# Residual of all eight groups on DVE, with x loaded into SBUF a second time and no adding transfers

## The chip, the cores and the metric

The kernel runs on one core of a Trainium2 chip. Its time is the device time of one execution in microseconds (us); the median of several executions is compared. Profiles come from one execution each. The engines are TensorE (PE in the rows), VectorE (DVE), ScalarE (ACT), GpSimd (POOL) and SyncE (SP), which here only issues transfers.

## What is computed

The input x is 4 sequences of 512 tokens with 256 channels, f32. It is normalised, goes through a recurrent attention layer (RWKV: the WKV scan over time) and a mixture of 16 experts of which each token uses 4, and the product of both is added to x:

```python
x = L0_attn_hidden                    # (4, 512, 256)
xn = _layernorm(x, axis=-1)
s = _L0_attn_ref(xn, ...)             # k, v, r = projections of mixed xn; s = (r * wkv) @ Wo.T
g = _silu(_L0_ffn_ref(xn, ...))       # sum over the 4 chosen experts of coeff * (silu(x Wg) * (x Wu)) @ Wd
x = x + s * g
```

## The kernel before

**Stages.** x is loaded and normalised in SBUF (in the room of `rT`), stored as rows to DRAM (`xn_rows`), projected to k, v and r (`kT`, `vT`, `rT`), and routed: a table says which row of which token goes to which expert and in which order. Then the loop over units of 256 rows runs. `NEED` = 32 units always, up to 14 more by the counts; here 36 run. For one unit i:

- POOL gathers 2 x 128 rows from `xn_rows` (`gather`, line 388) and, `LAG` = 6 units behind, scatters 2 x 128 finished rows into `y_rows` (`scatter`, line 395). `y_rows` has one section for each of a token's four chosen experts, called slots.
- TensorE transposes the rows (`transpose_x`), makes gate and up products (`gate_up`) and the down products of an earlier unit (`down`). `product` is line 584, so all of these have that line in the profile.
- ScalarE copies out the transposed rows (`evac_x`), applies Silu (`silu`, line 534), loads the weights of the next unit's expert (`load_weights`, line 442) and copies y (`evac_y`, line 544). `evac_y(i)` waits until the scatter of unit i - 2 from the same buffer has landed (`y_out`). After eight units (`EXPS_AT`) it also does one Exp of 128x2048 for WKV, between `evac_x` and `silu` of its step.
- DVE multiplies gate and up (`hidden`, line 1022) and in between works off the WKV scan in pieces (`WKV_AT`); the last piece is done in step 29. `wkv_ready` counts the eight pieces (4 sequences x 2 halves of the channels).

k's room is free for other data once the WKV of its columns is done; `xre` are eight views of [128, 2, 256] into `kT`, one for each group of two token tiles.

**The end.** For each token the four slots are read back from `y_rows` into `y4` and summed with their weights into `acc`. The reads are issued by SP in order: slot 0 in one transfer (line 304), slot 1 in halves (308), slot 2 in quarters (313), slot 3 in eighths (321), each as soon as the counts say that its rows have been scattered. DVE sums: slot 0 at line 1087, the others at 1089, through `weighted` and `summed`; the `hidden` of the last two units stand between the sums of slots 0 and 1. After the last read, for each of the eight groups n: DVE adds slot 3 (`weighted(n, 3)`), ScalarE applies Silu (line 577), DVE multiplies by s, which TensorE left in PSUM (`gated`, line 1119).

x is added in two ways. Groups 0 to 5 (`ADDED`): early in the loop, after two WKV pieces, SP copies their x from the input to the output in DRAM (line 294), and at the end POOL stores `acc` with transfers that add to what is there (line 431). Groups 6 and 7 (`SUMMED`): SP loads their x into `xre` behind the reads of slot 2 (line 316), DVE adds it (`residual`, line 1126), and SP stores the result (line 324). The kernel ends when both kinds of stores have landed (lines 325 and 326).

## Time and profile before

| | |
|---|---|
| median of 3 executions | 328.44 us (327.49 to 329.75) |
| the profiled execution | 325.01 us |
| its span, first to last instruction | 323.3 us |
| busy: PE, PEld, DVE, ACT, POOL | 286.9, 210.9, 250.4, 146.1, 202.8 us |
| DMA | 63.27 MB, mean 196 GB/s |
| mean granted TensorE clock | 0.98 |

The span is the time between the first and the last instruction in the profile of one execution. An engine's busy share of it is an average over stages with different limits; which engine sets the end in a stage is read from its idle time and from who ends it. "Landing" is the time from the issue of a transfer to its completion.

### The profile page before, as it was taken

To read this page: it belongs to the slowest core of one execution; us is meant where nothing else is said; L and a number is where in the kernel's file an instruction comes from. 1 tells how busy PE (TensorE), PEld (TensorE's weight loads), DVE (VectorE), ACT (ScalarE), POOL (GpSimd) and SP (SyncE) were. 2 spreads that over 40 slices of the span, in tenths; PEclk is the share of its full clock that TensorE was granted. 3 is DMA by queue.
4 is the path that set the end of the run, shared out by engine and by line. 5 is a ranking of instruction groups with operands and counts; after the bars stand their busy time and mean duration, and the time that the engine had idled before them with its cause. 6 is when DMAs were issued, how large, how long until landed. Compare 5 with 4: busy or idle time off the path is not lost.

```text
span 323.3 us, 4531 instructions
## 1 busy us (share of the span) xinstructions
PE 286.9 (89%) x1298; PEld 210.9 (65%) x1299; DVE 250.4 (77%) x516; ACT 146.1 (45%) x219; POOL 202.8 (63%) x201
## 2 busy tenths in 40 slices
PE   0698969999899999999899999999999999998910
PEld 0433424444346657888788888888888888887800
DVE  2979799997886897697399886989869941196993
ACT  1792735423266934932836428273292323211040
POOL 3600079994872777587787777778777775425071
PEclk9999979999999999999999999999999999999995
DMA  7896000016298785677654646556465666996999
GB/s 234 278 396 266 0 1 1 0 57 230 86 262 269 277 290 152 215 222 255 194 188 148 209 138 207 182 170 205 149 214 158 167 223 183 388 300 216 307 213 180
DMA packets 30346, 63.27 MB, mean 196 GB/s; under 512 B 4300, under 2 KB 20173, under 8 KB 30160
## 3 DMA queue, kind: packets, MB, share of 16 engines
q10 hardware_dynamic: 7568, 23.88, 22.0%
q0 software_dynamic: 8544, 19.41, 21.4%
q1 hardware_dynamic: 14208, 19.66, 17.7%
q8 instruction: 13, 0.21, 0.3%
q14 instruction: 13, 0.11, 0.1%
HBM read 50.35 MB, written 15.20 MB: 203 GB/s over the span
## 4 chain that ended last, share of the span: by engine, by line
PE 62%; DVE 18%; DMA 10%; issue 4%; POOL 3%; ACT 1%; ACTq 0%; DVEq 0%; POOLq 0%; SPq 0%
PE ps L584 54%; PE ps L691 4%; DMA y_rows<-arena,late 4%; DVE arena L842 3%; DMA rows<-y_rows 3%; POOL arena L388 3%; DVE arena L1089 3%; DVE ohB L993 2%; PE ps L594 2%; DVE ohA L988 2%; DMA arena<-xn_rows,tok_idx 2%; DMA wrou<-wrouT_in 2%; DVE arena L1119 1%; PE ps L709 1%; DVE rows L817 1%
## 5 line engine op out<-in xcount | busy, mean ns | idle before, releaser
L584 PE MATMUL ps<-arena,rows 128*128 128x256 f32 x448 | 101.5, 380 | 0.7 <-issue 0.7
L388 POOL DMA_INDIRECT arena<-xn_rows,tok_idx x72 | 78.2, 1086 | 25.7 <-issue 21.7
L584 PEld LDWEIGHTS ps<-arena,rows 128*128 128x128 f32 x448 | 82.9, 190 | 11.4 <-issue 1.3
L395 POOL DMA_INDIRECT y_rows<-arena,dst_idx x60 | 66.6, 1110 | 25.7 <-issue 16.5
L584 PE MATMUL ps<-wdn,arena 128*128 x288 | 68.1, 380 | 2.4 <-DVE arena L1022 2.4
L584 PEld LDWEIGHTS ps<-wdn,arena 128*128 128x128 f32 x288 | 54.0, 190 | 10.2 <-issue 3.2
L584 PE MATMUL ps<-arena 128*128 128x512 f32 x96 | 47.2, 626 | 3.1 <-DVE arena L842 3.1
L544 ACT COPY arena<-ps 128x512 f32<-128x512 f32 x34 | 19.9, 587 | 64.1 <-PE ps L584 57.8
L370 POOL TENSOR_SCALAR ohB<-late 128x128 f16<-128x128 f32 x20 | 29.9, 1508 | 27.9 <-DVE late L918 27.3
L1022 DVE TENSOR_TENSOR arena<-arena,ps 128x512 f32<-128x512 f32 x28 | 19.1, 684 | 34.3 <-PE ps L584 15.0
L534 ACT ACTIVATE arena<-ps 128x512 f32<-128x512 f32 x36 | 21.5, 598 | 30.9 <-PE ps L584 30.8
L584 PEld LDWEIGHTS ps<-arena 128*128 128x128 f32 x96 | 17.4, 196 | 19.5 <-issue 15.2
L584 PE MATMUL ps<-rows,arena 128*128 128x512 f32 x64 | 29.0, 595 | 0.9 <-issue 0.7
L526 ACT COPY arena<-ps 128x512 f32<-128x512 f32 x36 | 21.5, 596 | 5.5 <-PE ps L691 5.0
L1089 DVE SCALAR_TENSOR_TENSOR arena<-rows,coef,arena 128x256 f32<-128x256 f32 x48 | 20.1, 480 | 3.7 <-DMA rows<-y_rows 3.6
L691 PE MATMUL ps<-ident,arena 128*128 128x128 f32 x144 | 21.6, 274 | 1.3 <-DMA arena<-xn_rows,tok_idx 1.3
L691 PEld LDWEIGHTS ps<-ident,arena 128*128 128x128 f32 x144 | 17.8, 141 | 6.2 <-issue 2.0
L584 PEld LDWEIGHTS ps<-rows,arena 128*128 128x128 f32 x64 | 11.5, 190 | 12.8 <-issue 12.1
L842 DVE SCALAR_TENSOR_TENSOR arena<-arena,vec 128x512 f32<-128x512 f32 x24 | 16.9, 742 | 0.0
L594 PE MATMUL ps<-ident,rT 128*128 128x128 f32 x32 | 6.8, 358 | 10.6 <-ACT rT L457 10.6
L474 ACT ACTIVATE arena<-arena,late 128x512 f32<-128x512 f32 x24 | 15.7, 718 | 0.0
L395 POOL DMA_INDIRECT y_rows<-arena,late x8 | 8.0, 1000 | 12.1 <-ACT arena L544 10.0
(179 smaller groups left out, 371.0 us busy)
## 6 DMA issues: line engine op xcount, KB each, us to landing
rows<-wgu_in ACTq DMA_DIRECT2D x44, 512.0 KB, 4.0
wdn<-wd_in SPq DMA_DIRECT2D x1, 4096.0 KB, 13.9
rT<-x_in SPq DMA_DIRECT2D x4, 512.0 KB, 6.0
xn_rows<-rT SPq DMA_DIRECT2D x4, 512.0 KB, 3.5
rows<-y_rows SPq DMA_DIRECT2D x1, 2048.0 KB, 10.6
rows<-y_rows SPq DMA_DIRECT2D x2, 1024.0 KB, 8.1
rows<-y_rows SPq DMA_DIRECT2D x4, 512.0 KB, 7.5
rows<-y_rows SPq DMA_DIRECT2D x8, 256.0 KB, 4.4
```

What stands on the lines that cost most here:

```text
L370: ins = pool.tensor_scalar(ohB[:, t % RING, s], iota_row, prow[:, t, s:s + 1], val[:, 1 - s % 2, t:t + 1], ALU.is_equal, ALU.mult)
L388: pool.indirect_dma_start(out=xg[i % XG][:, j, :], out_offset=None, in_=xn_rows, in_offset=bass.IndirectOffsetOnAxis(ap=tok_idx[:, 2 * i + ...
L395: pool.indirect_dma_start(out=y_rows, in_=ysb[:, par, j, :], in_offset=None, out_offset=bass.IndirectOffsetOnAxis(ap=idx[:, n + j:n + j + ...
L474: ins = nc.scalar.activation(mix[b % 2][w][:, c, :], xnT[:, c, b, 0:SEQ], ACT.Copy, scale=unmix[:, w * C + c:w * C + c + 1])
L526: nc.scalar.copy(xTg[:, i % 2].rearrange("p c t -> p (c t)"), ps[:, XT_BANK[i % 2], :]).then_inc(xt_ready, 1)
L534: nc.scalar.activation(dst, src, ACT.Silu).then_inc(sg_ready, 1)
L544: nc.scalar.copy(ysb[:, par].rearrange("p j n -> p (j n)"), ps[:, Y_BANK[par], :]).then_inc(y_ready, 1)
L584: ins = nc.tensor.matmul(dst, lhsT(c), rhs(c), start=(c == 0), stop=(c == C - 1))
L691: ins = nc.tensor.transpose(ps[:, XT_BANK[i % 2], (c * 2 + j) * P:(c * 2 + j + 1) * P], xg[i % XG][:, j, c * P:(c + 1) * P], ident[:, :])
L842: ins = V.scalar_tensor_tensor(out=mix[b % 2][w][:, c, :], in0=xnT[:, c, b, 1:SEQ + 1], scalar=vec[:, (2 + w) * C + c:(2 + w) * C + c + 1] ...
L1022: V.tensor_tensor(hT[:, par].rearrange("p h t -> p (h t)"), sg[:, par], ps[:, B_G + 2 * par + 1, :], ALU.mult).then_inc(h_ready, 1)
L1089: ins = V.scalar_tensor_tensor(out=acc[:, t, :], in0=y4[:, t, k, :], scalar=coef4[:, t, k:k + 1], in1=acc[:, t, :], op0=ALU.mult, op1=ALU.add)
```

## The change

- SP no longer copies x to the output. In the loop it now waits until all eight WKV pieces are done and then loads x of all eight groups into `xre` (eight transfers of 256 KB), ahead of the reads of slots 0 to 3. The loads of groups 6 and 7 behind slot 2 go.
- The counts are read into SP's registers ahead of this wait; the wait for WKV ahead of the reads of slot 2 goes, since the same wait now stands earlier.
- POOL does no adding transfers. DVE does `residual` for all groups, that of group n - 2 behind `gated(n - 1)`, and SP stores each of the eight groups when its residual is done.

```diff
--- before.py
+++ after.py
@@ -195,7 +195,7 @@
         LAST_Y_BANK = [(Y_BANK[FIRST % 2], B_XT), (Y_BANK[(FIRST - 1) % 2], B_HT)]
         XN_BANK = [(B_XT, B_Y), (B_HT, B_G + 3)]
         S_BANK = [B_G, B_G + 1, B_G + 2, B_G + 3, B_XT, B_HT, B_R, B_Y]
-        ADDED, SUMMED, QUARTERS = range(6), range(6, T // 2), 4
+        QUARTERS = 4
         logits = ps[:, B_R, 0:T * E].rearrange("p (t e) -> p t e", t=T)
         LG_BANK = [B_G, B_G + 1, B_G, B_G + 2]
         prefix = ps[:, B_Y, 0:(T + 1) * E].rearrange("p (t e) -> p t e", t=T + 1)
@@ -244,7 +244,7 @@
         xre_in = sem("xre_in")
         acc_ready, silu_ready, s_psum, ffn_times_s, res_ready = (
             sem("acc_ready"), sem("silu_ready"), sem("s_psum"), sem("ffn_times_s"), sem("res_ready"))
-        out_stored, out_added, x_in_out = sem("out_stored"), sem("out_added"), sem("x_in_out")
+        out_stored = sem("out_stored")
 
         def wait(eng, s, value):
 
@@ -289,14 +289,13 @@
             sp.dma_start(wdn[:, :, :, :].rearrange("p c e n -> p (c e n)"), wd_in).then_inc(wdn_in, 16)
             sp.wait_ge(slots_known, 3)
 
-            sp.wait_ge(wkv_ready, C)
-            halves = lambda a: a.rearrange("b s d -> (b s) d")[0:len(ADDED) * 2 * P]
-            sp.dma_start(halves(out), halves(x_in)).then_inc(x_in_out, 16)
-
             counts = [sp.value_load(slot_done[0:1, n:n + 1], min_val=1, max_val=32 * (NP // 2 + 1))
                       for n in range(2 * (TOPK - 1))]
             scattered = [sp.value_load(used[0:1, 3 + par:4 + par], min_val=32 * (NEED // 2), max_val=32 * (NP // 2 + 1))
                          for par in range(2)]
+            sp.wait_ge(wkv_ready, C * BATCH)
+            for n in range(T // 2):
+                sp.dma_start(xre[n], out_order(x_in)[:, 2 * n:2 * n + 2, :]).then_inc(xre_in, 16)
             for s in range(TOPK - 1):
                 for par in range(2):
                     sp.wait_ge(y_out[par], counts[2 * s + par])
@@ -307,23 +306,19 @@
                         tt = slice(q * T // 2, (q + 1) * T // 2)
                         sp.dma_start(y4[:, tt, s, :], y_v[:, tt, s, :]).then_inc(y_second_in[q], 16)
                 else:
-                    sp.wait_ge(wkv_ready, C * BATCH)
                     for q in range(QUARTERS):
                         tt = slice(q * TB, (q + 1) * TB)
                         sp.dma_start(y4[:, tt, s, :], y_v[:, tt, s, :]).then_inc(y_third_in[q], 16)
 
-            for n in SUMMED:
-                sp.dma_start(xre[n], out_order(x_in)[:, 2 * n:2 * n + 2, :]).then_inc(xre_in, 16)
             sp.wait_ge(last_y_psum, 2 * 2)
             for par in range(2):
                 sp.wait_ge(y_out[par], scattered[par])
             for n in range(T // 2):
                 sp.dma_start(y4[:, 2 * n:2 * n + 2, TOPK - 1, :], y_v[:, 2 * n:2 * n + 2, TOPK - 1, :]).then_inc(y_last_in[n], 16)
-            for n in SUMMED:
-                sp.wait_ge(res_ready, n - SUMMED[0] + 1)
+            for n in range(T // 2):
+                sp.wait_ge(res_ready, n + 1)
                 sp.dma_start(out_v[:, 2 * n:2 * n + 2, :], acc[:, 2 * n:2 * n + 2, :]).then_inc(out_stored, 16)
-            sp.wait_ge(out_stored, 16 * len(SUMMED))
-            sp.wait_ge(out_added, 16 * len(ADDED))
+            sp.wait_ge(out_stored, 16 * (T // 2))
 
         @block.gpsimd
         def _(pool):
@@ -424,11 +419,6 @@
                     pool.indirect_dma_start(out=y_rows, in_=ysb[:, (FIRST + n) % 2, j, :], in_offset=None,
                                             out_offset=bass.IndirectOffsetOnAxis(ap=e_idx[:, column:column + 1], axis=0),
                                             bounds_check=last_row, oob_is_err=False).then_inc(y_out[(FIRST + n) % 2], 16)
-
-            pool.wait_ge(x_in_out, 16)
-            for n in ADDED:
-                pool.wait_ge(ffn_times_s, n + 1)
-                pool.dma_start(out_v[:, 2 * n:2 * n + 2, :], acc[:, 2 * n:2 * n + 2, :], accum_op=ALU.add).then_inc(out_added, 16)
 
         @block.scalar
         def _(act):
@@ -1122,7 +1112,7 @@
             def residual(n):
                 tt = slice(2 * n, 2 * n + 2)
                 dve.wait_ge(ffn_times_s, n + 1)
-                dve.wait_ge(xre_in, 16 * len(SUMMED))
+                dve.wait_ge(xre_in, 16 * (T // 2))
                 V.tensor_tensor(acc[:, tt, :], acc[:, tt, :], xre[n], ALU.add).then_inc(res_ready, 1)
 
             for n in groups:
@@ -1130,7 +1120,7 @@
                 weighted(n, TOPK - 1).then_inc(acc_ready, 1)
                 if n > 0:
                     gated(n - 1)
-                if n - 2 in SUMMED:
+                if n > 1:
                     residual(n - 2)
             residual(T // 2 - 2)
             gated(T // 2 - 1)
```

## Rows read from the trace of the kernel before

**Rows 1.** The page, part 4: chain that ended last, by engine

```profile
PE 62%; DVE 18%; DMA 10%; issue 4%; POOL 3%; ACT 1%; ACTq 0%; DVEq 0%; POOLq 0%; SPq 0%
```

**Rows 2.** Timeline of TensorE: start us, us, operation, count [idle before <-releaser]

```profile
146.66 1.89 PE L584 MATMUL ps<-wdn,arena 128*128 x8
...
159.25 1.99 PE L584 MATMUL ps<-wdn,arena 128*128 x8 [1.18 <-DVE arena L1022]
...
273.89 3.62 PE L584 MATMUL ps<-arena,rows 128*128 128x256 f32 x16
...
280.19 3.69 PE L584 MATMUL ps<-arena,rows 128*128 128x256 f32 x16 [0.52 <-issue]
```

**Rows 3.** Timeline of ScalarE, its copy of y (line 544) near 152 us

```profile
152.12 0.58 ACT L544 COPY arena<-ps 128x512 f32<-128x512 f32 x1 [6.39 <-DMA y_rows<-arena,dst_idx]
```

**Rows 4.** Line 395 (scatters), issued 120 to 140, then 142 to 145 us: landing

```profile
DMA to landing us min/median/max: 2.4/2.7/3.2
...
DMA to landing us min/median/max: 7.7/7.9/8.0
```

**Rows 5.** Timeline of SP's queue, whole span: issues (issue time, not landing)

```profile
141.37 0.63 SPq L294 DMA_DIRECT2D out<-x_in  x1
...
271.58 0.37 SPq L304 DMA_DIRECT2D rows<-y_rows  x1
...
292.58 2.61 SPq L313 DMA_DIRECT2D rows<-y_rows  x4
295.23 2.71 SPq L316 DMA_DIRECT2D kT<-x_in  x2
```

**Rows 6.** Timeline of DVE: end of WKV, weighted sums, last groups

```profile
260.52 0.69 DVE L1072 TENSOR_TENSOR rT<-arena,rT 128x512 f32<-128x512 f32 x1
...
286.99 0.69 DVE L1022 TENSOR_TENSOR arena<-arena,ps 128x512 f32<-128x512 f32 x1 [0.30 <-DVE arena L1087]
...
288.15 3.26 DVE L1089 SCALAR_TENSOR_TENSOR arena<-rows,coef,arena 128x256 f32<-128x256 f32 x8 [0.47 <-DMA rows<-y_rows]
...
298.49 6.83 DVE L1089 SCALAR_TENSOR_TENSOR arena<-rows,coef,arena 128x256 f32<-128x256 f32 x16 [2.95 <-DMA rows<-y_rows]
...
305.51 1.67 DVE L1089 SCALAR_TENSOR_TENSOR arena<-rows,coef,arena 128x256 f32<-128x256 f32 x4 [0.18 <-DMA rows<-y_rows]
...
309.09 0.88 DVE L1089 SCALAR_TENSOR_TENSOR arena<-rows,coef,arena 128x256 f32<-128x256 f32 x2
...
310.48 0.87 DVE L1089 SCALAR_TENSOR_TENSOR arena<-rows,coef,arena 128x256 f32<-128x256 f32 x2
...
316.15 0.69 DVE L1126 TENSOR_TENSOR arena<-arena,kT 128x512 f32<-128x512 f32 x1
...
316.76 0.68 DVE L1119 TENSOR_TENSOR arena<-arena,ps 128x512 f32<-128x512 f32 x1
...
317.47 0.69 DVE L1126 TENSOR_TENSOR arena<-arena,kT 128x512 f32<-128x512 f32 x1
```

**Rows 7.** Waits of SP's queue: us in total, times, longest

```profile
SPq L56 <- DMA out<-arena: 1.2, 1, 1.2
```

**Rows 8.** Landings: line 304; 442 at 267 and 272.6 us; 324; 288

```profile
rows<-y_rows SPq DMA_DIRECT2D x1, 2048.0 KB, 10.6
...
DMA to landing us min/median/max: 4.0/4.0/4.0
...
DMA to landing us min/median/max: 7.5/7.5/7.5
...
DMA to landing us min/median/max: 4.0/4.3/4.6
...
DMA to landing us min/median/max: 2.9/3.5/4.1
```

**Rows 9.** Stretches by engine: busy (x instructions), PEclk, DMA share, GB/s

```profile
266.00:270.00 4.00, 4.00 (x22) 3.52 (x21) 0.69 (x1) 1.07 (x2) 2.77 (x4) 1.00 0.63 196
...
278.00:282.00 4.00, 3.48 (x19) 2.89 (x18) 0.29 (x1) 1.07 (x2) 1.04 (x2) 1.00 1.06 385
```

## The prediction

> **What bounds the kernel now.** I read the page first: its part 4 puts TensorE on the path for most of the span, 62% of the chain that ended last [rows 1]. So I split the time in two. Through the expert loop, up to about 280 us, what moves TensorE moves the end. After that the chain hands over to DVE, and there I read the timeline of DVE and of SP's queue.
>
> The reader is to see three things. First, TensorE has almost no idle time in the loop. One of its gaps is the 1.18 us before the down products at 159.25 us, released by DVE line 1022 [rows 2]. Following that wait backwards: `hidden` waited for ScalarE's Silu, and ScalarE had stood still for 6.39 us before its copy of y at 152.12 us, released by a scatter into `y_rows` [rows 3]. An Exp (`EXPS_AT`) then came between that copy and the Silu. The two scatters issued from 142.4 us landed after 7.7 and 8.0 us, where those of the 20 us before needed 2.4 to 3.2 [rows 4]. What was new is the copy of x to `out`, issued at 141.37 us [rows 5].
>
> Second, at the end DVE is full. The third term's sums start at 298.49 us, when their first quarter lands, and run 6.83 us to 305.3; after that one group follows the other every 1.39 us (309.09 to 310.48), which is its two weighted sums and its gating and nothing else. Only groups 6 and 7 have a residual there, and the last ends at 317.47 + 0.69 = 318.16 us [rows 6].
>
> Third, what follows is SP's: its last wait for a store takes 1.2 us [rows 7]. I take it for that of group 7, which lands 4.0 us after its issue [rows 8], at about 318.2 + 4.0 = 322.2 of the 323.3 us. Then the adding transfers are over before it and end nothing.
>
> **The change, part by part.** *Copy of x removed.* The 1.5 MB from x to `out` at 141.37 us goes. The wait of ScalarE behind the scatter was what held the loop up, and scatters of 2.4 to 3.2 us would have landed by 147.5 us, ahead of the y product that the copy of y needs, done at 146.66 + 1.89 = 148.55 us [rows 2]. So the 1.18 us of TensorE come back, and since it then runs without a gap until about 280 us, all later work comes earlier by it: **-1.2 us**. Bounds: 0, if something else on ScalarE's way held it as long; the whole gap, rounded up, -1.3. That POOL's scatters move with TensorE I assume.
>
> *Six more residuals on DVE.* POOL's six adding transfers go; DVE does six more `tensor_tensor` of 128x512 f32. The trace has the same operation twice, 0.69 us each [rows 6]. In a chain with no wait, though, the next instruction starts before the former has ended: the gating at 316.76 starts 0.61 us after the residual at 316.15, and 1.39 less two weighted sums of 3.26/8 = 0.41 us each leaves 0.57 us for a gating [rows 6]. I take 0.60 us: 6 x 0.60 = 3.6 us. Nothing hides it, DVE being full from 298.5 us on. From this goes 0.1 us, because residual(6) no longer stands right behind the gating that it needs: **+3.5 us**. Bounds 3.4 (six of 0.57) and 4.1 (six of 0.69). The Trainium skill (VectorE: DVE Perf Modes, The TRN2 errata) gives a fp32 `tensor_tensor` (N + 151)/0.96 ns, 691 ns for 512 elements, and says that SBUF latency is exposed between instructions; by that the term would be 4.1 us, the sum 0.6 us more. The 0.69 of single instructions here agrees, the spacing does not, and I go by the spacing.
>
> *x loaded earlier.* All eight groups (2 MB, eight issues) now go out once WKV is done, 260.52 + 0.69 = 261.2 us, ahead of the read of the first term, which was issued at 271.58 us [rows 5, 6]. Both move earlier with TensorE, so the room of 10.4 us stays. Eight issues take 8 x 1.36 = 10.8 us if each is as slow as the two of line 316, and 8 x 0.65 = 5.2 us by the four of line 313 [rows 5]. So SP is hardly late. What is queued behind on SP is the reads of the first, second and third term and then of the last. As to the engines: between 266 and 270 us the DMA moves 196 GB/s at a share of 0.63, and 385 at 1.06 when it is full [rows 9], so some 189 GB/s are free, and 2.1 MB need 11.1 us. About 1 us of backlog is left when the first term's read is issued. That read's landing after 10.6 us, at 282.2 [rows 8], lets DVE end `hidden` at 286.99 + 0.69 = 287.7, 0.47 us ahead of the second term's first half [rows 6], so half of it is slack. The rest is given back at the end, where 0.5 MB of x no longer lie between the third term and the last scatters (0.5 MB at 385 GB/s is 1.4 us).
>
> The weight loads feel it too. In the loop a load lands after 4.0 us, but the one issued at 272.6 us, beside the first term's read, took 7.5 [rows 8]: it landed at 280.1, and TensorE started its products at 280.19 us after 0.52 us idle [rows 2]. The one before, issued at 267.0 us for the products at 273.89, has 6.9 us; with x in the way as the first term was, it lands 0.6 us late: **+0.6 us**. Bounds: 0 (the x loads are over, or take only spare bandwidth) and 2.0 (0.6 for each of two loads and 0.8 on the first term's read).
>
> *x loads gone from 295.23 us.* They stood behind the third term on the same queue, so they delayed no sum of it. The last term's first read can come sooner, but DVE is busy until 305.3 us anyway; DVE's next sum started at 305.51, 0.2 us after it [rows 6]: **-0.1 us**, bounds -0.2 and 0.
>
> *Stores.* Each group goes out on SP when its residual is done, now one per 1.39 + 0.60 = 2.0 us. The last still follows the last residual. Before, it landed after 4.0 us beside adding transfers; the kernel's other stores, 512 KB to `xn_rows`, land after 2.9 to 4.1 us, median 3.5 [rows 8]. I take 3.3 us: **-0.7 us**; bounds -1.1 (2.9) and +0.6 (4.6, the other store of line 324). The Trainium skill (DMA: Bandwidth & Descriptors, Anatomy of one DMA) gives 2.0 us and bytes/436e3 for a DMA issued from GpSimd: 2.6 us for 256 KB, an estimate by which this term were -1.4 and the sum 0.7 us less. No store of this trace is that quick.
>
> Sum: -1.2 + 3.5 + 0.6 - 0.1 - 0.7 = +2.1 us. On the profiled execution's 325.01 us (a span of 323.3 and 1.7 around it) that is 327.1. The median shown, 328.44, is 3.4 us above the profiled one; the same +2.1 on it gives 330.5 us. Own range of this case, with the copy's term kept near -1.2: the low ends add up to +0.8; the high ones would make +5.5, but they hardly come together, and the largest of them (2.0 instead of 0.6) with half of the next (0.6) makes +4.1: 329.2 to 332.5.
>
> **The rivals.** *The stall stays (no gain from the copy's removal).* Against it speaks that the long landings begin with the copy; for it, that the wait was found in one execution only. Then +2.1 + 1.2 = +3.3, 331.7 us.
>
> *x ahead of the first term holds up the sums: slower.* Place: SP's queue at 272 us. If the eight issues take 10.8 us and the engines serve weights and scatters in turn with x, the first term's read begins 2 to 3 us late. Its sums, `hidden` of the last unit but one, the second term's first half, `hidden` of the last unit, its down products and its scatter follow each other on DVE and TensorE [rows 6]. Of a landing 2.9 us late 0.5 is slack and the last scatter's easier way gives back 0.6: 1.8 us more, +3.9, 332.3 us. It decides (over 1%, 3.3 us) from 1.2 us handed on, a landing 1.7 us late with nothing given back. For it: the full DMA from 274 us on, in which the first term's 2 MB take 10.6 us. Against it: 10.4 us of room.
>
> *The copy cost more than the profiled execution shows.* Once ScalarE's Silu is late, every further us of the scatters' landing is a us of TensorE, and the runs shown are 3.4 us slower than the profiled one. If 3 us come back: +0.3, 328.7 us; with a quicker last store it is faster than before.
>
> **How the numbers follow.** Forecast 0.60, the stall that stays 0.12, x ahead of the first term 0.18, the dearer copy 0.10. About 1% (3.3 us) is what a measurement of this kernel can tell from no change, its three runs being 2.3 us apart. Slower by over 1%: 0.05 of the forecast, half of the first rival, 0.15 of the second, together 0.26. Faster by over 1%: 0.04, all from the third. The rest, 0.70, is within 1%. The range runs from the third rival's lighter side, 328.0, to the second's heavier, 333.4, with a tenth or so left out in all.
>
> **What would show it.** In the profile after: no idle of ScalarE over 1 us for a scatter near 150 us, and no gap of TensorE at 158; scatters there land in about 3 us. DVE's groups at the end 2.0 us apart and eight residuals, with no wait for x between. The last residual ends at about 318.16 - 1.2 + 3.5 + 0.5 = 321.0 us. SP's x issues from about 260 us, the first term's read 10 us behind, one TensorE gap of about 0.5 us more near 273. A last store that lands in 3.3 us. The prediction is wrong if TensorE has new gaps of more than 1 us, if the first term lands over 1.7 us later relative to TensorE's steps, or if the residuals cost less than 0.5 us each because DVE waits for reads of the last term.

## The result, and the profile after

| | before | after |
|---|---|---|
| median of 18 executions each | 327.9 us (325.85 to 330.97) | 330.35 us (328.29 to 332.59) |
| ratio after / before | | 1.0097, 95% interval 1.0072 to 1.0122 |
| profiled execution's span | 323.3 us | 326.9 us |

The change makes the kernel slower by just under 1%. The ratios and their intervals, here and below, compare only executions of the faster of two groups that the executions of one kernel fall into, so they are not the quotients of the medians, which take in all; the profiles of early_copy and pe6_spread are of slower executions.

The forecast, 330.5 us, was met in the median. The rows below show that this is partly luck: the stores gained about 2 us more than forecast, the copy and the loads of x together did about 1 us worse, and about 0.9 us of the difference lies where the forecast has no term.

At the end, DVE's timeline of the kernel after (start us, us, operation, count, what ended the idle time before). Line 1079 is the weighted sum, 1109 the gating, 1116 the residual; they answer to lines 1089, 1119 and 1126 in [rows 6].

```profile
307.68 1.72 DVE L1079 SCALAR_TENSOR_TENSOR arena<-rows,coef,arena 128x256 f32<-128x256 f32 x4 [0.88 <-DMA rows<-y_rows]
...
310.35 0.88 DVE L1079 SCALAR_TENSOR_TENSOR arena<-rows,coef,arena 128x256 f32<-128x256 f32 x2 [0.35 <-DMA rows<-y_rows]
...
312.35 0.88 DVE L1079 SCALAR_TENSOR_TENSOR arena<-rows,coef,arena 128x256 f32<-128x256 f32 x2
313.14 0.68 DVE L1109 TENSOR_TENSOR arena<-arena,ps 128x512 f32<-128x512 f32 x1
313.74 0.68 DVE L1116 TENSOR_TENSOR arena<-arena,kT 128x512 f32<-128x512 f32 x1
314.34 0.87 DVE L1079 SCALAR_TENSOR_TENSOR arena<-rows,coef,arena 128x256 f32<-128x256 f32 x2
...
323.62 0.69 DVE L1116 TENSOR_TENSOR arena<-arena,kT 128x512 f32<-128x512 f32 x1
```

The groups now follow each other every 1.99 us (312.35 to 314.34), 0.60 us more than before, and the last residual ends at 324.31 us.

SP's last wait and the landing of its eight stores, after (the page's list of issues: count, KB each, median us to landing):

```profile
SPq L56 <- DMA out<-arena: 1.8, 1, 1.8
```
```profile
out<-arena SPq DMA_DIRECT2D x8, 256.0 KB, 2.1
```

The span ends 326.9 - 324.31 = 2.6 us after the last residual. In [rows 6, 7] it is 323.3 - 318.16 = 5.1 us.

TensorE's timeline after, near the place of the old gap, and at the last units:

```profile
159.93 1.89 PE L574 MATMUL ps<-wdn,arena 128*128 x8
...
274.50 3.69 PE L574 MATMUL ps<-arena,rows 128*128 128x256 f32 x16
...
287.57 3.71 PE L574 MATMUL ps<-arena,rows 128*128 128x256 f32 x16 [2.04 <-issue]
292.90 1.99 PE L574 MATMUL ps<-wdn,arena 128*128 x8 [1.61 <-DVE arena L1012]
```

The gap of 1.18 us in [rows 2] is gone. In front of the last unit's gate and up products there is a gap of 2.04 us, where the kernel before had 0.20.

The chain that ended last (the page, part 4) of the kernel after, and of before_again, which is the kernel before profiled once more:

```profile
POOL 32%; PE 21%; DVE 18%; DMA 13%; issue 12%; ACT 2%; ACTq 0%; POOLq 0%; SPq 0%; DVEq 0%
```
```profile
POOL 41%; PE 23%; issue 12%; DVE 11%; DMA 8%; ACT 2%; POOLq 0%; ACTq 0%; DVEq 0%; SPq 0%
```

In [rows 1] it was TensorE 62% and POOL 3%. So through the loop two chains are nearly as long as each other: TensorE's products, and POOL's queue of gathers and scatters, which from about 140 to 260 us never pauses for more than 0.31 us in any of these three profiles. Which of them ends last differs between two executions of the same kernel, and a gap of TensorE moves the end only where it is TensorE's.

Last, what the loads of x did, by ScalarE's waits (its copies of y, line 534) and the chain that ended last (start us, us, what), after:

```profile
269.91 0.59 ACT L534 COPY arena<-ps 128x512 f32<-128x512 f32 x1 [4.15 <-DMA y_rows<-arena,dst_idx]
...
274.66 0.59 ACT L534 COPY arena<-ps 128x512 f32<-128x512 f32 x1 [3.17 <-DMA y_rows<-arena,dst_idx]
```
```profile
263.54 6.29 DMA y_rows<-arena,dst_idx
...
269.91 0.59 ACT arena L534
...
271.30 3.35 DMA y_rows<-arena,late
274.65 12.38 DMA rows<-y_rows
...
287.05 4.64 DVE arena L1077 x16
```

A scatter issued at 263.54 us, beside the x loads that SP issued from 261.8 to 268.5 us, landed after 6.29 us. ScalarE waited for it with its copy of y, POOL could scatter that y only afterwards, and the first term's read was issued at 274.65 us, 6.1 us after SP had issued its last load of x. The gap of 2.04 us of TensorE does not stand in this chain.

Two executions of one kernel differ before the loop, in code that is the same in all of them: the double down products that stand at 139.32 us in the profile before came at 139.3 to 144.1 us in the kernels whose segments are compared below (at 141.35 in the one after). So I compare segments:

- **loop**: from the start of those double down products (16 matmuls) to the start of the last unit's gate and up products (285.81 us in the profile before)
- **sums**: from there to DVE's first sum of the last term (305.51)
- **groups**: from there to the end of the last residual (318.16)
- **out**: the rest of the span

| kernel | copy of x beside the loop | x into `xre` | loop | sums | groups | out |
|---|---|---|---|---|---|---|
| before | yes | two, behind third term | 146.5 | 19.7 | 12.7 | 5.1 |
| before_again | yes | same | 147.7 | 18.4 | 13.2 | 5.3 |
| before_plain | yes | same | 147.9 | 22.0 | 12.7 | 2.5 |
| before_nocopy | no | same | 144.9 | 19.8 | 12.7 | 5.6 |
| early_copy | no, issued at 18 us | same | 145.3 | 20.7 | 12.9 | 6.1 |
| after | no | eight at 261 us | 146.2 | 20.1 | 16.6 | 2.6 |
| after_again | no | same | 146.5 | 20.1 | 16.5 | 2.5 |
| after_two_res | no | same | 146.2 | 20.5 | 12.9 | 2.6 |
| after_copy | yes | same | 147.5 | 21.0 | 16.6 | 2.6 |
| after_spread | no | four parts | 145.1 | 20.8 | 16.3 | 2.5 |
| after_late_x | no | eight, behind third term | 145.4 | 24.2 | 16.2 | 2.6 |
| early_copy_add4 | no, issued at 18 us | four, two parts | 146.8 | 19.7 | 14.1 | 2.6 |

(In before_nocopy DVE does not pause between the third and the last term, so the line between its sums and groups is set 16 sums, 6.83 us, behind the first of them.) The mean of the two profiles after is 1.3 us above the mean of the first two before: loop -0.7, sums +1.1, groups +3.6, out -2.7. The border between loop and sums lies behind the gap in front of the last unit's products, which varies from 0 to 2.70 us; the two segments added up are steadier: 166.2 and 166.1 us before, 166.3 and 166.6 after. The medians differ by 2.5 us (2.1 for after_again beside its own kernel before); the ratio, 1.0097, stands for 3.2 us (2.4 to 4.0). Of what the segments leave out, 0.6 us is the mean difference ahead of the loop (139.32 and 141.15 us before, 141.35 and 140.26 after; chance can't be told from effect with two profiles each), and 0.3 us lies outside the span: an execution takes 1.7 to 1.8 us more than its span before, 1.9 to 2.2 after. That makes 2.2 us.

after_again is the kernel after once more, unaltered, in the company of the later variants; 1.008 to 1.010 of before was expected of it. It took 329.51 us, 1.0082 of before (1.0042 to 1.0122). Its profile repeats the gap of the last unit (1.91 us), ScalarE's two waits for scatters (4.34 and 3.09 us), the first read's landing after 12.4 us and the last store's after 2.1.

### The profile page after: what moved, and what is told of

It is laid out like the page before. It is cut to its first block, busy times and chain, and to the rows that moved or that the text cites. A ratio compares the mean times of both kernels' runs of the same rounds, so it can differ in the third digit from the quotient of the medians.

```text
span 326.9 us, 4545 instructions
## 1 busy us (share of the span) xinstructions
PE 286.8 (88%) x1298; PEld 210.8 (64%) x1299; DVE 253.8 (78%) x522; ACT 145.9 (45%) x219; POOL 195.8 (60%) x195
## 4 chain that ended last, share of the span: by engine, by line
POOL 32%; PE 21%; DVE 18%; DMA 13%; issue 12%; ACT 2%; ACTq 0%; POOLq 0%; SPq 0%; DVEq 0%
POOL arena L383 17%; PE ps L574 16%; POOL y_rows L390 15%; DMA rows<-y_rows 5%; DVE arena L832 3%; DMA y_rows<-arena,late 2%; DVE arena L1079 2%; DVE ohB L983 2%; DMA y_rows<-arena,dst_idx 2%; PE ps L584 2%; DMA arena<-xn_rows,tok_idx 2%; DVE ohA L978 2%; DMA wrou<-wrouT_in 1%; DVE arena L1077 1%; DVE arena L1109 1%
## 5 line engine op out<-in xcount | busy, mean ns | idle before, releaser
L390 POOL DMA_INDIRECT y_rows<-arena,dst_idx x60 | 65.6, 1094 | 25.4 <-issue 17.1
L365 POOL TENSOR_SCALAR ohB<-late 128x128 f16<-128x128 f32 x20 | 31.1, 1567 | 27.2 <-DVE late L908 26.5
L1079 DVE SCALAR_TENSOR_TENSOR arena<-rows,coef,arena 128x256 f32<-128x256 f32 x48 | 20.1, 478 | 1.4 <-DMA rows<-y_rows 1.2
L574 PEld LDWEIGHTS ps<-rows,arena 128*128 128x128 f32 x64 | 11.5, 190 | 12.9 <-issue 12.2
## 6 DMA issues: line engine op xcount, KB each, us to landing
rows<-y_rows SPq DMA_DIRECT2D x1, 2048.0 KB, 12.4
```

The costliest lines, as they stand in the source:

```text
L365: ins = pool.tensor_scalar(ohB[:, t % RING, s], iota_row, prow[:, t, s:s + 1], val[:, 1 - s % 2, t:t + 1], ALU.is_equal, ALU.mult)
L390: pool.indirect_dma_start(out=y_rows, in_=ysb[:, par, j, :], in_offset=None, out_offset=bass.IndirectOffsetOnAxis(ap=idx[:, n + j:n + j + ...
L574: ins = nc.tensor.matmul(dst, lhsT(c), rhs(c), start=(c == 0), stop=(c == C - 1))
L1079: ins = V.scalar_tensor_tensor(out=acc[:, t, :], in0=y4[:, t, k, :], scalar=coef4[:, t, k:k + 1], in1=acc[:, t, :], op0=ALU.mult, op1=ALU.add)
```

## The experiments

**Is it the copy of x that holds up the loop?** Two kernels, the copy added to the kernel after, and taken from the kernel before.

after_copy:

```diff
+            sp.wait_ge(wkv_ready, C)
+            sp.dma_start(x_copy, x_in.rearrange("b s d -> (b s) d")[0:6 * 2 * P]).then_inc(copied, 16)
...
             sp.wait_ge(out_stored, 16 * (T // 2))
+            sp.wait_ge(copied, 16)
```

> The changed kernel with one thing put back: 1.5 MB of x are again copied from DRAM to DRAM after two WKV pieces, now into a scratch tensor that nobody reads. Theory (the copy makes the scatters land late, ScalarE waits for them in front of an Exp, and TensorE idles): scatters issued beside it land after 6 to 8 us, ScalarE stands still for 4 us or more before the next copy of y, TensorE has a gap of 1.0 to 1.4 us some 15 us behind the copy, and the time is 1.3 us above the changed kernel's: 331.7 us, 1.014 of before. Rival (the copy is hidden, and the gap in the kernel before was something else): no gap, 330.4 us, 1.010 of before.

Measured: 330.03 us, 1.0052 of before (1.0011 to 1.0094). TensorE's timeline and the sum of ScalarE's waits for scatters (us in total, times, longest) of after_copy, the second also with the x loads in it:

```profile
162.69 1.99 PE L579 MATMUL ps<-wdn,arena 128*128 x8 [0.86 <-DVE arena L1017]
```
```profile
ACT arena L539 <- DMA y_rows<-arena,dst_idx: 13.7, 3, 6.1
```

The gap is back at its place, the longest wait is 6.1 us (before the copy of y at 155.56 us), and the loop takes 1.1 us more than in the two profiles after. The time does not show it: 1.014 was expected, the ratio is even below that of the kernel after, which wasn't run beside it, and the intervals overlap. In this profile too the chain that ended last runs through POOL (41%) and not through the gap, so a price of the gap in time need not show here. The stall is borne out, its price is not, by this run.

before_nocopy:

```diff
-            sp.dma_start(halves(out), halves(x_in)).then_inc(x_in_out, 16)
-            pool.wait_ge(x_in_out, 16)
```

> The kernel before without the copy of x to the output (groups 0 to 5 then lack x in what the adding transfers leave); the adding transfers stay. Theory (the copy costs TensorE 1.2 us through the late scatters, seen as gaps of 1.18, 0.79 and 1.95 us in three profiles with it): no gap near 160 us, time 1.2 us lower, 0.996 of before. Rival (what TensorE loses there is slack that the end's chain of scatters and reads takes back): 0.999 or more.

Measured: 325.47 us, 0.995 of before (0.992 to 0.9981), about 1.6 us. No gap of TensorE near 160 us, and a loop of 144.9 us. This puts the price in time between 0.6 and 2.6 us. The rival, that the end takes it back, falls, unless it matters to the adding transfers that nobody has written what they add to; early_copy writes it.

early_copy:

```diff
             sp.dma_start(wdn[:, :, :, :].rearrange("p c e n -> p (c e n)"), wd_in).then_inc(wdn_in, 16)
+            halves = lambda a: a.rearrange("b s d -> (b s) d")[0:len(ADDED) * 2 * P]
+            sp.dma_start(halves(out), halves(x_in)).then_inc(x_in_out, 16)
             sp.wait_ge(slots_known, 3)
-            sp.wait_ge(wkv_ready, C)
-            halves = lambda a: a.rearrange("b s d -> (b s) d")[0:len(ADDED) * 2 * P]
-            sp.dma_start(halves(out), halves(x_in)).then_inc(x_in_out, 16)
```

> The kernel before with one move: the copy of x to the output is issued right behind the load of the down weights, at about 17 us, and moves its bytes between 30 and 45 us, when the DMA of the kernel before carried next to nothing. Theory (the copy costs its 1.2 us only because it falls beside scatters in the loop): no gap of TensorE near 160 us, ScalarE waits for no scatter there, 1.2 to 1.7 us less than before, 0.995 of it. Rival (the 0.995 of the kernel without the copy came from the adding transfers reading an output nobody had written, or from chance): 1.000 of before.

Measured: 327.78 us, 0.9978 of before (0.9936 to 1.002). The copy was issued at 17.9 us and had landed by 34.5, ahead of the 45 us expected. No gap near 160 us, loop 145.3 us. The stall goes as expected, the time is unclear: both 0.995 and 1.000 lie in the interval. So that the late scatters are the copy's doing is shown; what this is worth at the end is 0.6 to 2.6 us by one kernel and not told from nothing by the other.

before_again, the kernel before once more for its profile:

> The kernel before once more, for its profile. Theory: TensorE's gap of about 1.2 us near 159 us, behind ScalarE's wait for scatters beside the copy of x, comes again, and the last store lands after about 4 us. Rival: the gap is missing in this execution, and was chance. The landing of the first term's read tells whether 10.6 us or the 12 us of the variants is usual.

Measured: one execution, 327.57 us. TensorE's gap came again, and the stores as before (timeline; list of issues):

```profile
160.68 1.99 PE L584 MATMUL ps<-wdn,arena 128*128 x8 [0.79 <-DVE arena L1022]
```
```profile
out<-arena POOLq DMA_DIRECT2D x6, 256.0 KB, 5.6
out<-arena SPq DMA_DIRECT2D x2, 256.0 KB, 4.2
```

The first term's read needed 12.2 us here, against 10.6 in [rows 8] and 12.4 in the kernel after. So the longer landing after is not the doing of x.

**What do the 2 MB at 261 us cost?**

after_spread:

```diff
-            sp.wait_ge(wkv_ready, C * BATCH)
             for n in range(T // 2):
+                if n % C == 0:
+                    sp.wait_ge(wkv_ready, C * (n // C + 1))
                 sp.dma_start(xre[n], out_order(x_in)[:, 2 * n:2 * n + 2, :]).then_inc(xre_in, 16)
```

> The changed kernel with x loaded in four parts of 0.5 MB, each as soon as the two WKV pieces of its sequence are done (at about 141, 180, 220 and 261 us), instead of 2 MB in one go at 261 us. Theory (the 2 MB in one go hold up the read of the first term, and the sums, scatters and last reads behind it follow): the first term's read lands 10.6 us or less after its issue instead of 12.4, the sums begin 1 to 2 us earlier relative to TensorE's steps, time 328.9 us, 1.005 of before. Rival (2 MB in one go cost nothing, the late sums of the changed kernel's profile are the spread between executions): 330.4 us, 1.010. A second rival: the part at 141 us falls where the copy of x was and brings back up to a third of its 1.3 us gap.

Measured: 328.47 us, 0.9992 of before (0.9939 to 1.0045). ScalarE waits for no scatter. The first term's read was issued 131.5 us behind the double down products, against 133.3 and 133.4 in the two profiles after, and landed after 12.2 us, as in them. So its sums begin 2 us earlier, as expected, but by the issue and not by the landing: what x in one go does is make scatters land late, which hold up ScalarE and the next scatters, and with them the read. Little of it reaches the end in the profile: loop and sums together take 165.9 us against 166.3 and 166.6. (The 1.2 us by which the loop alone is shorter lie in the gap in front of the last unit's products, 1.01 us here against 2.04 and 1.91.) The ratio shows more than the profile, 0.9992 against 1.0097 and 1.0082; where the rest of it lies stays open. The second rival, a gap from the first part at about 144 us, did not come.

after_late_x:

```diff
-            sp.wait_ge(wkv_ready, C * BATCH)
-            for n in range(T // 2):
-                sp.dma_start(xre[n], out_order(x_in)[:, 2 * n:2 * n + 2, :]).then_inc(xre_in, 16)
             for s in range(TOPK - 1):
...
+            for n in range(T // 2):
+                sp.dma_start(xre[n], out_order(x_in)[:, 2 * n:2 * n + 2, :]).then_inc(xre_in, 16)
             sp.wait_ge(last_y_psum, 2 * 2)
```

> The changed kernel with all eight x loads issued behind the reads of the third term, where the kernel before had two of them. Theory (in SP's queue what stands ahead delays what stands behind): the front is free again (first term's read lands after 10.6 us, a gain of 1 to 1.5 us), but the 2 MB lie ahead of the last term's reads, whose first lands 3 us later than it could: together 1.5 to 2 us above the changed kernel, 332.0 us, 1.015 of before. Rival (the place of the x loads does not matter as long as DMA keeps up): 330.4 us.

Measured: 331.8 us, 1.0066 of before (1.0025 to 1.0108), in the same session as after_spread, from which it is 3.3 us away in the median. DVE's timeline of after_late_x at the first sum of the last term:

```profile
311.29 1.67 DVE L1079 SCALAR_TENSOR_TENSOR arena<-rows,coef,arena 128x256 f32<-128x256 f32 x4 [5.14 <-DMA rows<-y_rows]
```

The last reads were issued at 305.39 us, and the first landed after 5.9 us, where 2.6 to 3.1 are usual. So the place of the loads matters as expected: ahead of the last reads they make DVE idle for 5.14 us, and loop and sums together take 169.6 us, 3.0 to 3.7 us more than with the loads in the loop. The size is not as expected: 1.015 lies outside the interval, and the ratio is below that of the kernel after, 1.0097, though the median is above its 330.35 us.

**What do the residuals cost?**

after_two_res:

```diff
+            wait_group = lambda n: sp.wait_ge(res_ready, n - 5) if n > 5 else sp.wait_ge(ffn_times_s, n + 1)
...
-                sp.wait_ge(res_ready, n + 1)
+                wait_group(n)
...
-                if n > 1:
-                    residual(n - 2)
```

> The changed kernel without the residuals of groups 0 to 5 (their output lacks x); their stores are issued when the gating is done. All x is still loaded. Theory (each residual costs DVE 0.6 us on the path to the end): groups on DVE 1.4 us apart instead of 2.0, time lower by 6 x 0.60 = 3.6 us, 326.7 us, 0.998 of before. Rival (the reads of the last term arrive every 1.4 us or slower and part of the residuals hides behind them): lower by 2.5 us or less, 327.9 us or more.

Measured: 325.31 us, 0.986 of before (0.9794 to 0.9927). Its groups on DVE:

```profile
310.95 0.88 DVE L1080 SCALAR_TENSOR_TENSOR arena<-rows,coef,arena 128x256 f32<-128x256 f32 x2 [0.16 <-DMA rows<-y_rows]
311.75 0.68 DVE L1110 TENSOR_TENSOR arena<-arena,ps 128x512 f32<-128x512 f32 x1
312.35 0.88 DVE L1080 SCALAR_TENSOR_TENSOR arena<-rows,coef,arena 128x256 f32<-128x256 f32 x2
```

1.40 us apart, and the segment of the groups is 12.9 us instead of 16.6 and 16.5: 3.6 us for six residuals, 0.60 each. Reads of the last term hide next to none of it. The time fell by more than that: 0.998 was expected, above the whole interval, and the median is 5.0 us below that of the kernel after. There are four executions, and what the rest is stays open; the 3.6 us stand on the profiles.

**Why does the end after the last residual take 2.6 us instead of 5.1?**

before_plain:

```diff
-    pool.dma_start(out_v[:, 2 * n:2 * n + 2, :], acc[:, 2 * n:2 * n + 2, :], accum_op=ALU.add).then_inc(out_added, 16)
+    pool.dma_start(out_v[:, 2 * n:2 * n + 2, :], acc[:, 2 * n:2 * n + 2, :]).then_inc(out_added, 16)
```

> The kernel before with POOL's six transfers at the end as plain stores instead of adding ones (groups 0 to 5 lack x in the output). Nothing else is altered, the copy of x is still made. Theory (adding transfers fill the DMA engines at the end and hold up SP's last store): the last store lands in 2.1 to 2.6 us instead of 4.0 and the time falls by 1.5 to 2 us, 0.995 of before. Rival (the store's 4.0 us has another cause, such as POOL's issues as such): it stays near 4 us and the time is that of before.

Measured: 326.65 us, 0.9966 of before (0.9922 to 1.001). The list of issues of before_plain, median landing last:

```profile
out<-arena POOLq DMA_DIRECT2D x6, 256.0 KB, 2.5
out<-arena SPq DMA_DIRECT2D x2, 256.0 KB, 2.1
```

With the same transfers issued by the same engine, only not adding, SP's last stores land after 2.1 us instead of 4.0 to 4.6, and the end takes 2.5 us. So it is the adding that holds up the plain stores beside it. The ratio shows 1.1 us less and not 2.6; its interval holds both -2.6 us and nothing. The gain at the end is shown by the profile, in the whole time it is not.

**Can another engine take the residuals?**

pool6_spread: x in four parts, and POOL, behind its last scatters, does (POOLED is 6)

```diff
+            pool.wait_ge(xre_in, 16 * (T // 2))
+            for n in range(POOLED):
+                tt = slice(2 * n, 2 * n + 2)
+                pool.wait_ge(ffn_times_s, n + 1)
+                pool.tensor_tensor(acc[:, tt, :], acc[:, tt, :], xre[n], ALU.add).then_inc(pool_res, 1)
```

> The changed kernel with two edits: x loaded in four parts as k's room comes free, and the residuals of groups 0 to 5 done by POOL, which is idle at the end; DVE keeps groups 6 and 7, SP stores all eight. Theory (DVE's residuals are what the change costs, and the quick plain stores and the removed copy are gains): DVE's groups are 1.4 us apart again, POOL needs 1.3 to 1.6 us for one residual and keeps up, the end is 3.6 us earlier than in the changed kernel with x in four parts: 325 us, 0.989 of before. Rival (POOL and DVE hinder each other when both read two SBUF operands, or POOL takes over 1.8 us each): POOL becomes the last, and the gain is 1.5 us or less: 327 us or more.

Measured: 332.14 us, 1.0143 of before (1.0066 to 1.0219). The timeline of pool6_spread at the end:

```profile
314.61 1.88 DVE L1087 SCALAR_TENSOR_TENSOR arena<-rows,coef,arena 128x256 f32<-128x256 f32 x2
314.77 1.44 POOL L429 TENSOR_TENSOR arena<-arena,kT 128x512 f32<-128x512 f32 x1 [1.35 <-DVE arena L1117]
...
316.42 0.68 DVE L1117 TENSOR_TENSOR arena<-arena,ps 128x512 f32<-128x512 f32 x1
...
317.01 1.88 DVE L1087 SCALAR_TENSOR_TENSOR arena<-rows,coef,arena 128x256 f32<-128x256 f32 x2
```

POOL would have kept up: 1.44 us a residual. But DVE's pair of weighted sums takes 1.88 us instead of 0.88, and the groups are 2.40 us apart, worse than with the residual on DVE. The weighted sum reads two operands in SBUF. The gating, which reads one of its two in PSUM, keeps its 0.68 us, but it never runs beside a residual of POOL, which starts when the gating has ended; so what POOL does to such an instruction is not shown. The Trainium skill (GPSIMD Engine Reference, Specifications) says that GpSimd shares its SBUF interfaces with VectorE and that they contend in instructions with two SBUF inputs; the 1.88 us of the pair agree.

pe6_spread: x in four parts, and TensorE adds, behind its products s (BY_PE is 6; the edit is shown without its reshaping of operands):

```diff
+            pe.wait_ge(xre_in, 16 * (T // 2))
+            for n in range(BY_PE):
+                pe.wait_ge(ffn_times_s, n + 1)
+                nc.tensor.matmul(ps[:, S_BANK[n], :], ident[:, :], xre[n], start=True, stop=False)
+                nc.tensor.matmul(ps[:, S_BANK[n], :], ident[:, :], acc[:, 2 * n:2 * n + 2, :], start=False, stop=True)
```

with ScalarE copying group n out behind the Silu of group n + 3.

> The changed kernel with x in four parts, and x of groups 0 to 5 added by TensorE: when group n is gated, two products with the identity put x and the gated group into its PSUM bank, ScalarE copies the sum out, SP stores it; DVE keeps the residuals of groups 6 and 7. Theory (DVE alone sets the end and TensorE and ScalarE have room there): DVE's groups are 1.4 us apart, each group costs TensorE 1.2 us at full clock and ScalarE 1.2 us, all under 1.4, and the end is 3.6 us earlier than with x in four parts on DVE: 325 us, 0.989 of before. Rival (the granted clock of TensorE falls at the end, as it did to 0.50 from 314 us in the kernel before, so a group costs it 2.4 us): groups on TensorE 2.4 us apart, the end not earlier than in the changed kernel, 328.5 us or more.

Measured: 328.03 us, 0.9991 of before (0.9943 to 1.004), no better than after_spread. TensorE's timeline of pe6_spread, and two stretches of it (busy of PE, PEld, DVE, ACT, POOL with instructions; granted clock; DMA share; GB/s):

```profile
313.54 1.02 PE L795 MATMUL ps<-kT,ident 128*128 128x512 f32 x2
...
315.26 1.02 PE L795 MATMUL ps<-kT,ident 128*128 128x512 f32 x2
```
```profile
316.00:320.00 4.00, 4.00 (x11) 1.73 (x10) 3.10 (x7) 2.80 (x6) 0.00 (x0) 1.00 0.39 131
320.00:324.00 4.00, 4.00 (x10) 1.50 (x8) 2.76 (x4) 1.71 (x4) 0.00 (x0) 1.00 0.42 143
```

Neither theory held. The clock stayed at 1.00, 2.4 GHz, while TensorE had work, so the rival's mechanism falls. But a group costs TensorE 1.72 us and not 1.2, and it could begin only at 313.54 us, behind the products s; so it finished after DVE, and ScalarE's copies, waiting for it, held up the Silu that DVE needed (idle of 0.24 to 0.47 us before the gating).

**A version better than both.**

early_copy_add4: early_copy, and new numbers of groups, with the x loads ahead of the reads:

```diff
-        ADDED, SUMMED, QUARTERS = range(6), range(6, T // 2), 4
+        ADDED, SUMMED, QUARTERS = range(4), range(4, T // 2), 4
...
+            for n in SUMMED:
+                if n % C == 0:
+                    sp.wait_ge(wkv_ready, C * (n // C + 1))
+                sp.dma_start(xre[n], out_order(x_in)[:, 2 * n:2 * n + 2, :]).then_inc(xre_in, 16)
```

> The same, and the groups divided anew: POOL's adding transfers for groups 0 to 3 (before: 0 to 5), residuals on DVE for 4 to 7, their x loaded in two parts, after the WKV of the third and of the fourth sequence. Theory (the adding transfers cost the end 2.6 us as long as the last of them lies beside SP's last store, a residual costs 0.6 us each): two more residuals +1.2 us, the last store lands in 2.1 to 2.6 us instead of 4 and ends alone, -2 to -2.6 us; in all 1.2 us below the kernel with only the early copy, 0.991 of before. Rival (the last adding transfer, issued at about 313 us, still slows the stores, or the x loads at 260 us cost the front 1 us): 0.995 or more.

Measured: 325.51 us, 0.9947 of before (0.9911 to 0.9982), beside early_copy at 0.9978. The list of issues of early_copy_add4:

```profile
out<-arena POOLq DMA_DIRECT2D x4, 256.0 KB, 5.4
out<-arena SPq DMA_DIRECT2D x4, 256.0 KB, 2.2
```

Two residuals more cost 1.2 to 1.4 us (groups 14.1 instead of 12.7 to 12.9), and the end behind them takes 2.6 us instead of 5.1 to 6.1, as the last adding transfer is over when the last store goes out. It is faster than both kernels of the change by its interval against before, by less than expected. That it is faster than early_copy is likely, not shown; the intervals overlap. Its profile has a gap of 2.70 us in front of the last unit's products, the largest of all.

## Why the prediction was right, point by point

**Copy removed, -1.2 us: right about the stall, only in part about the end.** TensorE's gap, ScalarE's wait and the late scatters are in all four profiles with the copy (gaps of 1.18, 0.79, 1.95 and 0.86 us) and in none of those without it. In time before_nocopy gave 0.6 to 2.6 us. Less its gaps of TensorE the loop takes 144.1 to 144.4 us in the profiles without the copy and 144.6 in those with it (in before_plain the products behind the gap also took 1.3 us longer). So nearly all that differs between loops is this stall and the gaps in front of the last units, 0 to 2.7 us in all, which vary between executions of one kernel. The step that was not right is *since it then runs without a gap until about 280 us, all later work comes earlier by it*, with the assumption that POOL's scatters move with TensorE. In the profile before and in before_plain the chain runs over the gap. In before_again, after, after_again, after_spread and after_copy it runs over POOL's queue from 140 us on, which has no gap to give back.

**Six residuals, +3.5 us: right.** 3.6 us by after_two_res, 3.6 by the segments (in the profiles, as said above). The spacing in the row, 0.60 us, was the measure to take, not the 0.69 of the single instruction.

**x earlier, +0.6 us: the size near, by another way than told.** I had priced a late weight load (0.6 us) and a backlog in front of the first term's read. The trace shows neither as the cause: the weights issued at 267.6 us landed after 6.9 us, and TensorE began its products at 274.50 with next to no gap; SP had issued all of x by 268.5 us, and the first read took about as long in profiles without x ahead of it (12.2 and 12.1 us in after_spread and after_late_x). What was late were the scatters beside x, 5.6 to 6.5 us instead of 3.4 to 4.0, the very mechanism that I had read off the copy of x and did not carry over to this load. ScalarE stood still for 4.15 and 3.17 us, and the first read was issued 1.6 to 2.0 us later relative to the double down products than in before_again and after_spread. At the last term's first sum 0.2 to 0.7 us of it were left, since DVE waited less for the third term. Against before_nocopy, whose first read landed after 10.5 us, it is 1.6 to 1.9 us; so the size is between 0.2 and 1.9 us. Two of the signs that I had named for a wrong prediction did come: a new gap of TensorE of more than 1 us, 2.04 and 1.91 us in front of the last unit's products, and a first term that lands over 1.7 us later relative to TensorE's steps, 2.8 us later than in the profile before and 1.8 later than in before_again. The gap remains open: the profile names the weights as awaited, yet they had landed 2 us earlier, and the gap also stands at 0.2 to 1.3 us in kernels before and at 2.70 in early_copy_add4.

**x gone from 295 us, -0.1 us: as good as right.** Nothing in the sums can be put down to it.

**Stores, -0.7 us: the term mis-sized.** It measured -2.6 to -2.7 us. The step that failed was to take for the new landing a value near the stores of 512 KB at the start, 3.3 us, when those are twice as large and ran beside other transfers (a DMA share of 0.68 from 12 to 16 us, 1.29 from 16 to 20). The adding transfers made a store of 256 KB land after 4.0 to 4.6 us; without them it lands after 2.1 (before_plain). In *What bounds the kernel now* I said that the adding transfers end nothing: as to their own landing that was so, but they set how long the store that did end the kernel took. The estimate from the Trainium skill (DMA: Bandwidth & Descriptors, Anatomy of one DMA), 2.6 us, was nearer than my row, and still above the 2.1 us measured; by it the sum would have been 0.7 us lower, at +1.4 us, near the +1.3 of the segments.

**The sum.** -1.2 + 3.5 + 0.6 - 0.1 - 0.7 = +2.1 us was forecast. The segments give +0.3 instead of -0.7 us for the three terms ahead of the groups (the copy, x earlier, x gone; 166.5 us in the mean against 166.2), +3.6 for the residuals and -2.7 for the stores, together +1.3 with rounding. The medians say +2.1 to +2.5, because 0.6 us more lie ahead of the loop and 0.3 outside the span, for which I had no term. So the mechanism of the largest term was right, and that the sum met the number is in part luck: the stores gained 2.0 us more than forecast, the copy and x together came out 1.0 worse, and 0.9 came from elsewhere. By the ratio, 2.4 to 4.0 us, the change costs a little more than I forecast, and 1.1 us or more of that is in no segment.

**The rivals.** That the stall stays is refuted (no gap in any profile without the copy). That x holds up the sums was right in kind: the first term landed 1.8 us later than in before_again, but because its read was issued late and not by SP's queue, and most of it was slack. (Against the profile before it is 2.8 us; the 1.0 us more is that profile's quick landing of 10.6 us, which before_again did not repeat.) That the copy costs more than the profile shows can't be excluded by before_nocopy's interval, but it did not turn the sign.

## What to carry to other kernels

A transfer that nobody waits for is not free: ask which small transfers run beside it, who waits for those, and with how much slack, and do it again for every new bulk load, also the one that replaces the first. Here 1.5 MB of copy and 2 MB of loads made scatters of 128 rows land up to 3 and 1.6 times as late, and each stopped ScalarE for 3 to 7 us. A single profile can show one of two chains that are nearly as long as each other: here TensorE had 62% of the chain in one profile of the kernel before and 23% in the next, and closing a gap on one of them can be worth less than its length. Read the landing of the last store beside what else is in flight, and let adding transfers end before it goes out; a hand-over of work to an idle engine is worth testing alone, since both takers tried here hindered the engine they were to relieve.

## What was unexpected in the hardware

- Six adding transfers of 256 KB at the end doubled the landing of plain stores beside them: 4.0 to 4.6 us against 2.1 us, while the same six as plain stores landed after 2.5 us instead of 5.6 to 5.9.
- A residual of POOL with two SBUF inputs (1.44 us) stretched DVE's pair of sums beside it from 0.88 to 1.88 us.
- The granted clock at the end was high while TensorE worked and fell after it had stopped. It was 1.00 in the stretches of pe6_spread above, in which TensorE was busy throughout; in the kernel before, whose TensorE had ended its last product by 308.4 us, it was 0.50 (1.2 GHz) from 314 us on, by the same view:

```profile
314.00:318.00 4.00, 0.00 (x0) 0.00 (x0) 3.93 (x8) 1.26 (x2) 2.02 (x2) 0.50 1.22 181
```
